# Six stages on one core: routing and transfers by groups of tokens, and a results tensor loaded in token order

## The reference

```
mixture (f0: 8 experts, hidden 176, shared hidden 352; f1: 16 experts, 128, 128)
  scores = sigmoid(x @ gate)            # T x E
  idx    = top_k(scores + bias, 2)
  w      = scores[idx] / sum(scores[idx])
  out    = sum_k w_k * ((silu(x @ W1[idx_k]) * (x @ W3[idx_k])) @ W2[idx_k])
         + (silu(x @ s1) * (x @ s3)) @ s2
recurrence (h)
  gate = sigmoid(x @ Wf); i = silu(x @ Wi) * (1 - gate)
  o    = scan over the tokens: o_t = gate_t * o_(t-1) + i_t
  out  = (g * rsqrt(mean(g^2) + eps) * norm * silu(o)) @ Wo,  g = x @ Wg
attention (a): 4 heads of 64, softmax(q k^T / 2) v @ Wo + bo, q, k, v with biases
```

## Time and profile before

| | |
|---|---|
| median of 3 runs | 1083.5 us (1081.2 to 1085.2) |
| profiled execution | 1087.4 us, its span 1085.5 us |
| TensorE products, weight loads | 814.8 us (75%), 546.9 us (50%) |
| VectorE, ScalarE, GpSimd | 468.2, 370.5, 360.0 us (43%, 34%, 33%) |
| granted clock of TensorE, mean | 0.88 of full speed (2.4 GHz) |

### The profile page before, as it was taken

How to read it: one execution, slowest core, us unless ns; L and a number is a source line. 1 busy time by engine, 2 the same in 40 slices (tenths; PEclk the granted TensorE clock), 3 DMA queues, 4 the chain that set the end, 5 groups by cost and what they waited for, 6 DMA issues and landing times.

```text
span 1085.5 us, 13666 instructions
## 1 busy us (share of the span) xinstructions
PE 814.8 (75%) x3674; PEld 546.9 (50%) x3675; DVE 468.2 (43%) x1388; ACT 370.5 (34%) x1012; POOL 360.0 (33%) x378
## 2 busy tenths in 40 slices
PE   5966999917997948999737459962699968349990
PEld 2333777703563426777513248851477743228870
DVE  4712222247565603322275522226666674612224
ACT  3200133335534100333243015544365533005552
POOL 0371033350000660233341745545000000744555
PEclk9987999967998979999959669995899989759995
DMA  8941133150000121233290234425000000234438
GB/s 286 314 150 63 44 108 107 64 174 0 1 1 1 63 92 40 90 105 95 81 357 15 87 126 149 152 89 149 1 1 1 1 0 1 83 120 143 151 106 242
DMA packets 79775, 104.54 MB, mean 96 GB/s; under 512 B 10422, under 2 KB 68150, under 8 KB 79158
## 3 DMA queue, kind: packets, MB, share of 16 engines
q1 hardware_dynamic: 65318, 64.51, 19.5%
q0 software_dynamic: 14400, 39.34, 10.2%
HBM read 56.23 MB, written 47.58 MB: 96 GB/s over the span
## 4 chain that ended last, share of the span: by engine, by line
PE 65%; DVE 11%; issue 8%; ACT 5%; DMA 4%; SPq 3%; another core or an unknown queue 2%; POOL 1%; DVEq 0%; ACTq 0%
PE bank L804 16%; PE bank L823 10%; PE bank L717 8%; PE bank L728 6%; PE bank L860 4%; PE bank L779 3%; PE bank L704 3%; PE bank L813 3%; PE bank L911 3%; DMA XT<-f_result_rows 2%; PE bank L685 2%; SPq L393 2%; PE bank L945 2%; PE bank L972 2%; ACT XT L472 2%
## 5 line engine op out<-in xcount | busy, mean ns | idle before, releaser
L413 POOL DMA_INDIRECT f_result_rows<-arena x172 | 164.8, 958 | 290.2 <-ACT arena L524 267.3
L413 POOL DMA_INDIRECT slot_rows<-XN,slots x128 | 139.0, 1086 | 313.5 <-DVE slots L1146 275.7
L804 PE MATMUL bank<-w,arena 128*128 x688 | 203.6, 418 | 6.9 <-issue 4.7
L1243 DVE COPY arena<-bank 88x128 f32<-88x128 f32 (+1 forms) x250 | 65.2, 285 | 243.5 <-PE bank L813 228.0
L804 PEld LDWEIGHTS bank<-w,arena 128*128 128x128 f32 x688 | 129.2, 190 | 41.2 <-issue 11.7
L823 PE MATMUL bank<-w,arena 88*128 (+1 forms) x500 | 136.5, 381 | 0.0
L728 PE MATMUL bank<-f_s,arena 128*128 128x256 f32 (+1 forms) x256 | 75.4, 449 | 69.8 <-DVE X L1201 46.5
L717 PE MATMUL bank<-XT,f_s 128*128 128x512 f32 (+1 forms) x256 | 120.9, 626 | 8.5 <-issue 6.1
L685 PE MATMUL bank<-ident,XN 128*128 128x128 f32 x192 | 40.9, 329 | 111.7 <-DVE XN L1064 97.0
L511 ACT ACTIVATE arena<-bank 128x256 f32<-128x256 f32 x172 | 65.8, 384 | 101.7 <-PE bank L779 100.9
L728 PEld LDWEIGHTS bank<-f_s,arena 128*128 128x128 f32 (+1 forms) x256 | 54.1, 221 | 92.1 <-DVE X L1201 51.0
(11 more groups left out here) (133 smaller groups left out, 1043.1 us busy)
## 6 DMA issues: line engine op xcount, KB each, us to landing
arena<-slot_rows SPq DMA_DIRECT2D x172, 128.0 KB
XN<-f_result_rows SPq DMA_DIRECT2D x16, 512.0 KB, 6.0
XT<-f_result_rows SPq DMA_DIRECT2D x32, 256.0 KB, 6.4
slot_rows<-zeros SPq DMA_DIRECT2D x1, 6016.0 KB, 20.2
w<-in_f_w SPq DMA_DIRECT2D x1, 4096.0 KB, 14.8
w<-in_f_w SPq DMA_DIRECT2D x1, 2816.0 KB
f_result_rows<-arena POOLq DMA_INDIRECT x172
X<-in_x SPq DMA_DIRECT2D x4, 512.0 KB, 5.1
```

What stands on the lines that cost most here:

```text
L413: pool.indirect_dma_start(out=dst, out_offset=bass.IndirectOffsetOnAxis(ap=idx, axis=0), in_=src, in_offset=None).then_inc(done.sem, 16)
L804: last = pe.matmul(bank[2 + q % 2][:, 0:2 * m.H], xsT[q % 2][:, k, :], L["w13"][:, k, bass.ds(e, 1), :], start=(k == 0), stop=(k == KD - 1))
L1243: last = dve.tensor_copy(hT[q % 2][0:kp, k, :], bank[4 + q % 2][0:kp, k * P:(k + 1) * P])
```

## The change

Nothing of what is computed changes. What is altered:

- Each expert has a region of 2176 rows of its own in x_rows, so that a token's slot is the expert's first row and its rank there. Ranks are made group by group: `positions(g)` and `place(g)` with a `carry` of the counts. GpSimd scatters a group after its `slotted`.
- SyncE fills 128 rows behind each expert's last row with zeros, at addresses loaded from memory into its registers, and loads the blocks of rows at addresses from a list `f_start` that VectorE makes in `tile_lists`. The fill of 6 MB is gone.
- A mixture's head goes by groups on all engines: `choose(g)` in place of `choices`, the sigmoid in `score(g)`, shared products between the groups (two a group in f0, one in f1), transposes through one bank. The logits of a group are products of 128 columns in four column groups of the array.
- ScalarE normalises, with a scale and a shift that VectorE makes in `scales`.
- `close_slots` turns the slots into closed ones for the `mark`s; marks, `slot_tokens` and `rows` follow behind, and TensorE waits for `rows` before the first block. `weights` comes after the experts.
- Second results are loaded into a new tensor Y2, which also holds the marks. `combine` is two operations a tile on VectorE; ScalarE's `weight` and GpSimd's sum are gone. GpSimd adds `abo`.
- In h and a groups arrive one by one: TensorE begins with the first. The attention's loop is written out, `arriving(b)` gives the group that comes in at a step, and xTb is gone.

The diff, cut to its core and less indented by eight columns (lines of "..." mark what is left out; `s["gathers"]` is False in all stages):

```diff
+Y2 = sb("Y2", [P, NTT, D])
...
+for k in range(2):
...
-    for g in range(NG):
-        sp.wait_ge(x_in[g], 16)
-    sp.wait_ge(zeros_set, 1)
-    sp.dma_start(x_rows.rearrange("(n p) d -> p n d", p=P),
-                 zeros[:, :].unsqueeze(1).broadcast_to((P, MOE1.TILES, D))).then_inc(rows_set, 16)
...
-        sp.wait_ge(*s["rows_out"](16 * 2 * NTT))
-        sp.wait_ge(*s["map_psum"](1))
...
+        sp.wait_ge(*s["ends"](1))
+        _, ends = nc.values_load_multi_w_load_instructions(
...
+        for e in range(E):
+            sp.dma_start(x_rows[bass.ds(ends[e], P), :], zeros[:, :]).then_inc(s["filled"].sem, 16)
+        def starts(j, n):
+            _, held["rows"] = nc.values_load_multi_w_load_instructions(
...
         def load_rows(j, q, r):
...
             if after(j, R):
                 sp.wait_ge(*s["r_xT_psum"](j - R + 1))
-            sp.dma_start(xs[q], x_rows[bass.ds(j * P, P), :]).then_inc(s["row_in"][q].sem, 16)
...
-        for g in range(NG):
...
+            sp.dma_start(xs[q], x_rows[bass.ds(row, P), :]).then_inc(s["row_in"][q].sem, 16)
+        sp.wait_ge(*s["starts"](1))
+        sp.wait_ge(*s["filled"](16 * E))
+        sp.wait_ge(*s["rows_out"](16 * 2 * NTT))
+        rounds(sp, tiles, load_rows, ahead=starts)
+        if not s["gathers"]:
...
+            for g in range(NG):
+                sp.dma_start(XN[:, g * GT:(g + 1) * GT, :], first[g]).then_inc(s["y_in"][g].sem, 16)
+                sp.dma_start(Y2[:, g * GT:(g + 1) * GT, :], second[g]).then_inc(s["y_in"][g].sem, 16)
...
+        for g in range(NG):
+            pool.wait_ge(*s["slotted"](g + 1))
+            for i in range(GT * g, GT * (g + 1)):
+                for k in range(2):
+                    scatter(x_rows, slots[:, k, i:i + 1], XN[:, i, :], s["rows_out"])
+        if not s["gathers"]:
+            pool.wait_ge(*s["rows"](1))
...
-        pool.wait_ge(*s["shared_added"](NTT))
-        for i in range(NTT):
...
-            pool.wait_ge(*s["weighted1"](i + 1))
-            pool.tensor_tensor(X[:, i, :], XN[:, i, :], X[:, i, :], ALU.add).then_inc(s["combined1"].sem, 1)
...
+        follows = stages[n + 1] if n + 1 < len(stages) else None
+        if follows and follows["kind"] == "a":
+            for g in range(NG):
...
+                pool.wait_ge(*follows["xn"](GT * (g + 1)))
+                pool.tensor_tensor(X[:, span, :], X[:, span, :], abo[:, :].unsqueeze(1).broadcast_to((P, GT, D)),
+                                   ALU.add).then_inc(follows["bo"].sem, 1)
...
+    def normalise(s, g):
+        act.wait_ge(*s["shift"](g + 1))
+        for i in range(GT * g, GT * (g + 1)):
+            act.activation(XN[:, i, :], X[:, i, :], ACT.Identity, scale=rs[:, i:i + 1],
+                           bias=shift[:, i:i + 1]).then_inc(s["xn"].sem, 1)
...
+        per = 2 if nk > 1 else 1
+        stdev(s, 0)
         for g in range(NG):
-            weight(s["prev"], g)
-        stdev(s, 0)
-        stdev(s, 1)
-        for g in range(NG):
+            normalise(s, g)
             for t in range(GT):
-                copy_xT(s, g, t)
-            if g + 2 < NG:
-                stdev(s, g + 2)
+                copy_xT(s, g, t, banks=1)
             logits(g)
-        act.wait_ge(*s["lg_psum"](NG))
-        act.activation(f_score[:, 0:NTT * m.E], bank[7][:, 0:NTT * m.E], ACT.Sigmoid).then_inc(s["scored"].sem, 1)
-        shared_silu(0, NG * nk)
+            score(g)
+            shared_silu(per * g)
+            if g + 1 < NG:
+                stdev(s, g + 1)
+            if per > 1:
+                shared_silu(per * g + 1)
+        for n in range(per * NG, NG * nk):
+            shared_silu(n)
...
+                for t in range(GT):
+                    last = pe.matmul(bank[6][t * Q:(t + 1) * Q, 0:P], L["router"][:, k, :],
+                                     XT[:, k, (GT * g + t) * P:(GT * g + t + 1) * P],
+                                     start=(k == 0), stop=(k == KD - 1))
...
+        per = 2 if nk > 1 else 1
         for g in range(NG):
+            if g:
+                positions(g - 1)
             for t in range(GT):
-                transpose_x(s, g, t)
-            if g:
-                logits_back(g - 1)
+                transpose_x(s, g, t, banks=1)
             logits(g)
-        logits_back(NG - 1)
-        loaded(pe, s["kind"] + "_shared")
-        shared_up(0, 2)
-        positions()
-        shared_up(2, 3 * nk)
-        pe.wait_ge(*s["scored"](1))
+            logits_back(g)
+            for n in range(per * g, per * (g + 1)):
+                shared_up(n)
+        positions(NG - 1)
+        pe.wait_ge(*s["scored"](NG))
+        if nk > 1:
+            shared_up(per * NG)
         shared_down(0)
-        slot_tokens()
-        shared_up(3 * nk, 4 * nk)
+        for n in range(per * NG + 1, NG * nk):
+            shared_up(n)
         for g in range(1, NG):
             shared_down(g)
+        if not s["gathers"]:
+            slot_tokens()
...
+        if not s["gathers"]:
+            pe.wait_ge(*s["rows"](1))
...
+        for i in range(GT * g, GT * (g + 1)):
+            dve.scalar_tensor_tensor(X[:, i, :], XN[:, i, :], wts[:, 0, i:i + 1], X[:, i, :],
+                                     ALU.mult, ALU.add).then_inc(s["combined1"].sem, 1)
         for i in range(GT * g, GT * (g + 1)):
             dve.wait_ge(*s["combined1"](i + 1))
...
+            dve.scalar_tensor_tensor(X[:, i, :], Y2[:, i, :], wts[:, 1, i:i + 1], X[:, i, :],
...
+    def scales(s, g):
...
+        dve.wait_ge(*s["stdev"](g + 1))
+        dve.reciprocal(rs[:, span], sd[:, span]).then_inc(s["rstd"].sem, 1)
+        dve.wait_ge(*s["rstd"](g + 1))
+        dve.scalar_tensor_tensor(shift[:, span], mv[:, span, 0], -1.0, rs[:, span],
+                                 ALU.mult, ALU.mult).then_inc(s["shift"].sem, 1)
...
+        def choose(g):
...
+            if g == 0:
+                loaded(dve, s["kind"] + "_router")
+                chain(dve.memset(f_m16[:, :, GT * E:(GT + 1) * E], 0.0))
+            dve.wait_ge(*s["scored"](g + 1))
+            chain(dve.tensor_tensor(sel, by_expert(f_score, g), L["bias"][:, :].unsqueeze(1).broadcast_to((P, GT, E)),
+                                    ALU.add))
             for k in range(2):
...
+                top, least, one = f_top[:, k, span], f_sum[:, span], by_expert(f_oh[k], g)
                 chain(dve.tensor_reduce(top, sel, AX.X, ALU.max))
                 chain(dve.tensor_tensor(tmp, sel, over_experts(top), ALU.is_equal))
...
+                chain(dve.tensor_tensor(tmp, tmp, numbers, ALU.mult))
+                chain(dve.tensor_reduce(least, tmp, AX.X, ALU.min))
+                chain(dve.tensor_tensor(one, numbers, over_experts(least), ALU.is_equal))
...
+        def place(g):
...
+            dve.wait_ge(*s["pos_psum"](g + 1))
+            ranks = bank[1][:, 0:GT * E].rearrange("p (t e) -> p t e", e=E)
+            chain(dve.tensor_tensor(pos, ranks, carry(g).unsqueeze(1).broadcast_to((P, GT, E)), ALU.add))
+            for k in range(2):
+                chain(dve.tensor_tensor(tmp, by_expert(f_oh[k], g), pos, ALU.mult))
+                chain(dve.tensor_reduce(f_slotf[:, k, span], tmp, AX.X, ALU.add))
+            dve.tensor_copy(slots[:, :, span], f_slotf[:, :, span]).then_inc(s["slotted"].sem, 1)
+            chain(dve.tensor_tensor(f_carry[(g + 1) % 2][:, 0:E], carry(g), bank[1][:, GT * E:(GT + 1) * E], ALU.add))
+        def tile_lists():
...
+            dve.tensor_copy(f_end[:, 0:E], carry(NG)).then_inc(s["ends"].sem, 1)
+            chain(dve.scalar_tensor_tensor(f_cnt[:, 0:E], carry(NG), float(P - 1), region[:, 0:E], ALU.add, ALU.subtract))
+            chain(dve.tensor_scalar(tiles_i, f_cnt[:, 0:E], 7, None, ALU.arith_shift_right))
+            chain(dve.tensor_copy(tiles_f, tiles_i))
+            chain(dve.tensor_tensor_scan(cum, ones[:, 0:E], tiles_f, 0.0, ALU.mult, ALU.add))
+            chain(dve.tensor_tensor(ge, iota[:, 0:NT].unsqueeze(2).broadcast_to((P, NT, E)),
+                                    cum.unsqueeze(1).broadcast_to((P, NT, E)), ALU.is_ge))
+            chain(dve.tensor_reduce(eidf, ge, AX.X, ALU.add))
+            dve.tensor_scalar(f_eid[:, 0:NT], eidf, float(E - 1), None, ALU.min).then_inc(s["experts"].sem, 1)
+            chain(dve.tensor_tensor(ge, ge, tiles_f.unsqueeze(1).broadcast_to((P, NT, E)), ALU.mult))
+            chain(dve.tensor_reduce(first, ge, AX.X, ALU.add))
+            chain(dve.scalar_tensor_tensor(first, eidf, float(SPACE // P), first, ALU.mult, ALU.subtract))
+            chain(dve.tensor_tensor(first, first, iota[:, 0:NT], ALU.add))
+            chain(dve.scalar_tensor_tensor(first, first, float(E * SPACE // P), first, ALU.is_lt, ALU.mult))
+            chain(dve.tensor_scalar(first, first, float(P), None, ALU.mult))
+            dve.tensor_copy(f_start[:, 0:NT], first).then_inc(s["starts"].sem, 1)
...
+        def close_slots():
...
             chain(dve.tensor_tensor(base, cum, tiles_f, ALU.subtract))
...
```

(55 more changed lines are left out.)

472 lines of the change are left out of this document (227 added, 245 removed).

## The result

The changed kernel took 1139.1 us (median of 4 runs, 1138.4 to 1143.1) against 1082.6 us for the kernel before: a ratio of 1.053, 95% interval 1.049 to 1.056. The profiled execution has a span of 1141.2 us, 55.7 more than before. The sign was as forecast; the size was not: 1102 with a range up to 1128 was given, and the sum had +18.4 us.

A forecast was written before the change was run, and what follows sets the result against it. The prediction took the heads and seams between stages as the case, with f0 heads bound by TensorE and f1 heads by slots, then scatters. Its terms summed to +18.4 us, giving 1105.8, as a median 1102 us; the range was 1060 to 1128.

The forecast's parts named there:

- The heads' cycle and its clock: Mixture heads: a group takes 17.7 us in f0 and 16.4 in f1, 3 us of each for a lower TensorE clock.
- VectorE's tail in f1: End of the f1 heads: VectorE's list work after the last slots takes 34.3 us.
- The recurrence: Seam into the recurrence: projecting starts 13.6 us earlier, most of it given back, -3.5 us (0 to -10).
- The f1 heads: Heads of the two f1 mixtures: +8 us for the first and +13 us for the last.
- The end: End of the kernel: VectorE's two operations a tile take 13.6 us against 13.0 us before, -1.5 us.
- The clock rival: Mixture heads: TensorE stays at 2.4 GHz, each of 12 later cycles 3 us shorter, 1066 us; chance 28 in 100.
- The attention: Attention: scores(1,0) comes 18.5 us earlier, arriving groups give back part, -9 us (-16 to 0).
- the price of an arrival: Attention loop: each of three arriving groups makes TensorE wait 3.8 us behind ScalarE's queue, 11.4 us in all.
- the second f0's head: Head of the second f0 mixture: 116.2 us against 111.8, +4.4 us, with none of the 18 us of issue stalls.
- The first f0: Head of the first f0 mixture: waits for f0_shared before its first transpose, +7 us.
- The expert loops: Expert loops of the mixtures: not altered in what they compute, so no term in the sum.
- the stall rival: Both f0 heads: TensorE's issue stalls stay as long as before, +36 us, 1138 us; chance 14 in 100.

The follow-up runs named there:

- changed_again: The changed kernel, unedited, run again on another chip than the first: 1115.5 us, 1.066 of the kernel before on the same chip.
- filled_turns: The changed kernel with products nobody reads put into TensorE's waits in a mixture's head: 1077.8 us, 1.029 of the kernel before.
- before_again: The kernel before, unedited, traced on another chip than the first: 1050.1 us in a single execution.
- att_upfront: The changed kernel with all attention groups combined, measured and normalised before the loop: 1104.5 us, 1.057 of the kernel before.
- att_ahead: att_upfront with square roots taken earlier, VectorE not waiting for each, and GpSimd's bias addition after the last normalise: 1103.5 us, 1.054 of the kernel before.
- short_tail: The changed kernel with low halves of marks made by groups and TensorE waiting for rows only at the second tile's hidden: 1086.0 us, 1.037 of the kernel before.

## Why the prediction was wrong

*What held.* The heads' cycle and its clock: 16.4 us a group in f1 and 17.7 in f0 were forecast, 15.8 to 17.2 and 16.7 to 19.0 measured on the first chip, 15.0 to 16.4 and 16.9 to 17.4 in changed_again; without the clock's fall 13.4 was forecast for f1 and 12.8 to 14.6 measured in filled_turns. That the first chip's 17.2 is so near to 16.4 is in part luck: 1.4 us of it are a stall that the sum didn't have, and the clock was charged at 3 us where some 2 came back. VectorE's tail in f1: 34.3 (its terms add up to 34.5) and 33 us. The recurrence: -3.5 (its terms give -3.2) and -2.2. The f1 heads: +8 and +13 forecast, +8.2 and +13.9 measured; changed_again against before_again has +5.8 and +13.6. The end: -1.5 forecast, -2.6 measured. But its stated terms, 13.6 against 13.0 us, don't give -1.5. By the traces the combine takes 12.8 us (13.6 before), and it begins 5.5 us after the first load's issue, not 7.5. The clock rival, at 28 in 100, was too likely: the earlier trace rows showed just the alternation that came.

*The attention* (-9 forecast, +8.4 measured) is the largest miss, and the step that failed is the price of an arrival. Starting early gave what was said (first scores 12 us sooner after the load of results, and scores(1,0) 18.0 sooner, where 18.5 were forecast). But an arriving group was priced at 3.8 us, from ScalarE's queue, with TensorE behind its transposes; VectorE's 5 us of combine and moments, which the same arrival puts ahead of the next maxima, weren't in the sum, and ScalarE's block was counted without the copies and the second table load that stand between the normalise and the next exponential. Measured against the 6.65 us at which scores come elsewhere: 4 us for VectorE's and 6 for ScalarE's block, 9.1 to 10.7 an arrival, 30 in all instead of 11.4. On the other chips the attention from the load of results takes 164.0 us against 157.7 before, and in att_upfront and att_ahead, which have no arrivals in the loop, 154.0 and 152.6: so the arrivals are what turned a gain into a loss.

*The issue stalls.* The sum had "none of the 18 us" left in f0, and the rival put all 36 us back. Both were wrong in kind: the changed kernel kept 22 us of the stalls on the first chip, spread over 12 cycles (1.4 us behind the logits in most) and the tails of f0 (3.3 us each). In changed_again the second f0's head takes 115.4 us, against the forecast's 116.2: the whole miss of that head is the stalls. The first f0 is at 128.2 there, against 122.5 + 7 = 129.5. That the rival's 1138 is near the measured 1139 is chance: 22 us of it were there, and the attention made up the rest.

Set against changed_again, which has no such stalls, the forecast's own parts show the same without them: they sum to 12 us less than its trace, of which the attention is 17.7 too low and the f0 loops 4.4, while the heads are 10 too high, 4.5 of it in the first f1. The rest nearly cancels. So the attention's term failed on either chip; the kernel before, from whose times all differences were counted, had 44 us of stalls of its own.

*The expert loops.* That they aren't altered was taken as costing nothing. They are entered from a sparse tail and a wait of 1.7 us, at a clock of 0.83 or 0.66 instead of 1.00 or 0.96, and are 2.1, 2.0, 0.4 and 3.3 us longer. In f0 that is the change: the loops take 101.7 to 101.8 us in both traces of the kernel before, 103.8 to 104.1 in both of the changed one, and 102.0 to 102.1 in short_tail without the wait. In f1 it isn't shown to be: before_again enters its f1 loops at 0.72 and 0.60 and takes 89.5 and 90.0 us for them, changed_again at 1.00 and 0.83 and takes 87.1 and 87.9. There the clock at the entry differs from one run to the next with either kernel.

*The range* reached 1128, and "most of the stall rival" was left out of it. It held no case in which the attention loses.

## What to carry to other kernels

When a step is moved into a loop, price it on every engine that it touches, at the place where each takes it, and not only on the engine whose queue was looked at. In a chain by groups, look first at whether the next group's first steps run under this group's long product: here they didn't, and each cycle held the wait for them (3.2 us in f1) and some 2 us for the clock's fall. And a stage that isn't altered still depends on the clock at which it is entered.

## What the runs showed of the hardware

- In the first runs TensorE stands between products while GpSimd scatters tokens (1.2 us between products of 0.2 us in `slot_tokens`, 1.4 us more behind the logits), though not through all of the scatters; on three chips it doesn't. The kernel before takes 1083 us in the one case and 1046 to 1048 in the others. The cause is open.
- Products that nobody reads made the changed kernel 3% faster: the last head's granted clock went from 0.67 to 0.83, and its shared product from 4.5 to 5.9 us to 3.60.
- GpSimd additions of SBUF tensors (2.3 to 2.4 us each) held up the VectorE operations on SBUF that ran beside them: four additions took 3.76 us instead of 1.67, and two scalings 4.66 us instead of 0.62 beside two such additions.
- The f0 expert loops, with the same instructions, take 2 us longer when they are entered at a granted clock of 0.83 than at 1.00 (first 10 us).
